# Queries and keys computed by features instead of by tokens, rotated by GpSimd and brought to the operands by DMA

## Chip, cores and metric
The kernel runs on one core of one Trainium2 chip. The metric is the device time of one execution in microseconds. The kernel before was timed in three runs; a fourth execution was recorded by the profiler.

## What is computed
Two sequences of 1024 tokens of width 512 (float32) pass six residual steps: an FFN with a LoRA term and a column norm, grouped attention with a rotary embedding (32 query heads, 8 key heads, 16 dimensions), the FFN again, a top-2 mixture of eight LoRA experts, a second attention (8 heads of 32 dimensions), and the experts again. Each step begins with a layer norm.

```
x = x + 0.5 * _L0_ffn_ref(_layernorm(x), ...)
x = x + _L0_attn_ref(_layernorm(x), ...)
x = x + 0.5 * _L0_ffn_ref(_layernorm(x), ...)
x = x + 0.5 * _L1_ffn_ref(_layernorm(x), ...)
x = x + _L1_attn_ref(_layernorm(x), ...)
x = x + 0.5 * _L1_ffn_ref(_layernorm(x), ...)
```

The rotation of the first attention takes the dimensions 2d and 2d + 1 of a head, xr and xi, to xr * cos - xi * sin and xr * sin + xi * cos.

## The kernel before
Each sequence passes eight stages (FFN_A, QKV0, WO0, FFN_B, MOE_A, QKV1, WO1, MOE_B) in three chains, with the rotated attention A0 after QKV0 and the standard attention A1 after QKV1. Every engine's program is written out by hand, in order, and engines meet by semaphores. Nothing is reordered later.

A chain handles eight tiles of 128 tokens per stage, in ticks. In tick i TensorE turns the normalised tile i to features by tokens (`turn_x`, L576), and multiplies tile i - 1 (`product`, `three_passes`, L596 to L598). Operands are split in a high and a low part of fp32r, so that a product has three passes; ScalarE copies the high part of the turned tile (L1080), the vector engine subtracts the low part (`turned_lo`, L844), takes statistics two tiles ahead (L825, L827), normalises the next tile (L837) and adds the product to x (`epilogue`, L872 to L879). GpSimd computes the inverse deviation (`rstd_of`, L1222, L1224), splits the weights of the next stage (`split_chunk`, L1215) and adds a bias (`bias_x`, L1235). In a tick of the experts the vector engine also routes (L887 to L891) and weighs (`weigh`, L898 to L910).

In QKV0 and QKV1 a product is 128 tokens by 768 features (two halves of 384 columns, L596 to L598). The vector engine adds the bias (L864) into one of three buffers. For A0 it multiplies by the cosine (L919), GpSimd by the sine in two strided instructions (L1254), and the vector engine adds (`rope_sum`, L932). ScalarE writes the high parts twice into a stack of 64 columns per head (`high_parts`, L1116, L1119), GpSimd subtracts the low parts beside them (`low_parts`, L1288, L1290) and copies the values (L1263). TensorE then turns the stacks, four blocks of 128 columns at a time (`turn_piece`, L654; five pieces per tile in A0, four in A1), four ticks behind the product, and ScalarE takes each piece to the operands (`evacuate`, L1137). An operand holds, per head, rows for high, low and again high (48 rows in A0, 96 in A1), and two more rows for the shift of the softmax.

Attention works in units of heads (8 units of 4 heads in A0, 4 of 2 in A1). For each unit a ring of three PSUM banks carries score maxima (TensorE L674, vector engine L976 and L980), the transposed shifts (L679, L989) and the normalisation of the result (L684, L996, L1001). The ring runs about one unit ahead of the scores (L759 in A1, L765 in A0), exponentials (ScalarE L1180), causal masks (GpSimd L1333) and value products (L781). 27 maximum banks of A0 and 21 of A1 stand ahead of the first score, twelve and six of them inside the chain's last ticks (`begun`). SP issues all DMAs in one queue: the shift rows go from `shiftT` to the operands (L495), weights from a copy in memory (`load_weights`).

## Time and profile before
| | |
|---|---|
| median of 3 runs | 1405.7 us (1405.19 to 1406.45) |
| profiled execution | 1411.57 us, span 1409.8 us |
| busy in the span | TensorE 1286.9 (91%), vector engine 943.4 (67%), ScalarE 639.8 (45%), GpSimd 483.3 (34%) |
| chain that ended last | TensorE 69%, vector engine 16%, GpSimd 5%, issue 4%, ScalarE 4%, DMA 2% |
| mean granted clock of TensorE | 0.929 |
| DMA queue of SP | 19312 packets, 38.23 MB, 8.0% of 16 engines |

The span runs from the first to the last instruction. Busy time is a sum of durations; matmuls are pipelined, so that a duration is longer than the distance from one matmul to the next. A share of the whole span is a mean of stages with different limits: what a stage is worth is read from windows of time. The granted clock is a share of TensorE's full speed, 0.5 being the lower of its two levels (1.2 of 2.4 GHz).

### The profile page before, as it was taken

Reading aid. Unit: us, or ns where it says so; the run is one execution under the profiler, and the core shown is the slowest. Engines: PE = TensorE matmul, PEld = TensorE weight load, DVE = VectorE, ACT = ScalarE, POOL = GpSimd, SP = SyncE. Lnnn points to the kernel's source line nnn. Section 1 sums busy time; section 2 is a strip of 40 time slices with the busy share of each in tenths; the row PEclk is TensorE's granted clock in tenths of the full one; section 3 lists DMA queues with packets and bytes.
Section 4 is the critical chain, followed back from the end, with each engine's and each line's share of the span. In section 5 each row is a group of like instructions: output and inputs, shape, how many; then the busy total and the mean of one; then the engine's idle time right before and its main releaser. Section 6 shows DMA issues by size and latency. Waiting matters only on the chain.

```text
span 1409.8 us, 21535 instructions
## 1 busy us (share of the span) xinstructions
PE 1286.9 (91%) x7392; PEld 824.5 (58%) x7392; DVE 943.4 (67%) x2782; ACT 639.8 (45%) x959; POOL 483.3 (34%) x733
## 2 busy tenths in 40 slices
PE   3988999999899998998979889999998999999988
PEld 1886543444268896444858854444432788954368
DVE  5664888999337944652857468889991587366356
ACT  1236266666632335444212544666665222544522
POOL 1574031221155542114626621321122554311162
PEclk9999588999999999899989976999999999989999
DMA  9200000001002001000140000000010100010001
GB/s 300 92 1 30 2 2 2 32 3 40 1 1 71 1 1 39 2 2 0 61 145 1 1 31 2 2 4 31 2 40 2 57 16 1 3 37 1 2 0 60
DMA packets 19420, 39.60 MB, mean 28 GB/s; under 512 B 4401, under 2 KB 5681, under 8 KB 19185
## 3 DMA queue, kind: packets, MB, share of 16 engines
q1 hardware_dynamic: 19312, 38.23, 8.0%
q8 instruction: 60, 0.98, 0.3%
q14 instruction: 48, 0.39, 0.1%
HBM read 32.33 MB, written 11.29 MB: 31 GB/s over the span
## 4 chain that ended last, share of the span: by engine, by line
PE 69%; DVE 16%; POOL 5%; issue 4%; ACT 4%; DMA 2%; SPq 0%; DVEq 0%; ACTq 0%; POOLq 0%
PE bank L781 16%; PE bank L674 12%; PE bank L596 8%; PE bank L598 7%; PE bank L597 7%; DVE maxes L980 5%; PE bank L765 4%; PE bank L654 4%; PE bank L759 3%; PE bank L576 3%; DVE unused L976 3%; PE bank L684 2%; POOL probs L1254 1%; DVE xT L844 1%; DVE gate L904 1%
## 5 line engine op out<-in xcount | busy, mean ns | idle before, releaser
L1180 ACT ACTIVATE probs<-bank 128x1024 f32<-128x1024 f32 (+3 forms) x416 | 367.9, 911 | 304.3 <-PE bank L765 195.6
L674 PE MATMUL bank<-ops 48*128 48x512 f32 (+3 forms) x960 | 321.0, 438 | 13.2 <-DVE maxes L980 3.8
L976 DVE CUSTOM_DVE_ANT_0 unused<-bank,causal 128x128 bf16<-128x128 f32 (+3 forms) x640 | 279.5, 486 | 73.9 <-PE bank L674 70.5
L1333 POOL TENSOR_SCALAR_AFFINE_SELECT probs<-probs 128x256 f32<-128x256 f32 (+1 forms) x256 | 118.8, 464 | 590.1 <-ACT probs L1180 589.9
L674 PEld LDWEIGHTS bank<-ops 48*128 48x128 f32 (+1 forms) x960 | 162.5, 207 | 198.2 <-DVE maxes L976 81.6
L781 PE MATMUL bank<-probs,v_mem 128*17 128x512 f32 (+6 forms) x1920 | 259.1, 531 | 6.1 <-ACT heads_raw L1169 5.6
L980 DVE TENSOR_REDUCE maxes<-bank 128x1 f32<-128x512 f32 x320 | 207.2, 684 | 38.0 <-PE bank L674 36.4
L1080 ACT CAST xT<-bank 128x512 fp32r<-128x512 f32 (+1 forms) x128 | 71.3, 560 | 280.5 <-PE bank L576 280.5
L844 DVE TENSOR_TENSOR xT<-bank,xT 128x512 fp32r<-128x512 f32 (+1 forms) x128 | 83.6, 656 | 148.4 <-ACT xT L1080 148.4
L765 PE MATMUL bank<-ops 50*128 50x512 f32 (+2 forms) x640 | 177.9, 454 | 4.1 <-ACT probs L1180 4.0
L596 PE MATMUL bank<-w_odd_hi,xT 128*128 128x384 f32 (+2 forms) x448 | 169.0, 377 | 2.1 <-DVE xT L844 1.9
L598 PE MATMUL bank<-w_odd_hi,xT 128*128 128x384 f32 (+2 forms) x448 | 152.8, 341 | 0.0
L597 PE MATMUL bank<-w_odd_lo,xT 128*128 128x384 f32 (+2 forms) x448 | 152.6, 341 | 0.0
L765 PEld LDWEIGHTS bank<-ops 50*128 50x128 f32 x640 | 87.3, 199 | 60.7 <-ACT probs L1180 30.8
L596 PE MATMUL bank<-ops,xT 128*128 128x512 f32 (+1 forms) x288 | 114.3, 397 | 5.3 <-DVE x L877 3.4
L1137 ACT CAST ops<-bank 128x512 fp32r<-128x512 f32 x144 | 81.7, 587 | 67.4 <-PE bank L654 67.0
L1222 POOL TENSOR_SCALAR var_eps<-mv 128x1 f32<-128x1 f32 x96 | 34.8, 363 | 202.3 <-DVE mv L827 202.3
L598 PE MATMUL bank<-ops,xT 128*128 128x512 f32 (+1 forms) x288 | 104.0, 361 | 0.0
L597 PE MATMUL bank<-ops,xT 128*128 128x512 f32 (+1 forms) x288 | 103.7, 360 | 0.0
L654 PE MATMUL bank<-identf,features 128*128 128x128 f32 x512 | 80.0, 293 | 22.1 <-POOL heads_raw L1290 16.1
L596 PEld LDWEIGHTS bank<-w_odd_hi,xT 128*128 128x128 f32 x448 | 85.8, 192 | 7.7 <-DVE xT L844 2.4
L597 PEld LDWEIGHTS bank<-w_odd_lo,xT 128*128 128x128 f32 x448 | 86.0, 192 | 3.5
(102 smaller groups left out, 1743.6 us busy)
## 6 DMA issues: line engine op xcount, KB each, us to landing
w_odd_lo<-staging_wqkv SPq DMA_DIRECT2D x4, 1536.0 KB, 6.7
x<-x_dram SPq DMA_DIRECT2D x16, 256.0 KB, 6.0
out_dram<-x SPq DMA_DIRECT2D x16, 256.0 KB, 2.0
staging_wqkv<-wqkv_dram SPq DMA_DIRECT2D x2, 1536.0 KB, 14.1
ops<-staging_dora SPq DMA_DIRECT2D x3, 1024.0 KB, 5.1
ops<-staging_base SPq DMA_DIRECT2D x2, 1296.0 KB, 6.4
w_odd_lo<-staging_base SPq DMA_DIRECT2D x2, 1296.0 KB, 5.8
ops<-shiftT SPq DMA_DIRECT2D x160, 4.0 KB
```

Of the source, the lines that this page charges most:

```text
L596: mm(dst, x_hi[:, k, :], hi[:, k, :], start=(k == 0), stop=False)
L597: mm(dst, x_hi[:, k, :], lo[:, k, :], start=False, stop=False)
L598: last = mm(dst, x_lo[:, k, :], hi[:, k, :], start=False, stop=(k == kc - 1 and not lora))
L654: last = nc.tensor.transpose(dst[:, k * P:(k + 1) * P], src, identf[:])
L674: last = mm(dst[:, h * w:(h + 1) * w], queries(a, u)[rows, t // 4, hi, t % 4 * P:(t % 4 + 1) * P], keys(a, u, hi)[rows, HALF * kp:HALF * k ...
L765: last = mm(dst, keys(a, u, 0)[rows, block], queries(a, u)[rows, c, heads_of[0]:heads_of[-1] + 1, columns], start=True, stop=True)
L781: last = mm(heads[a.head_rows * h:a.head_rows * h + a.dim + 1, q0 - HALF * c:HALF], v[:, j, a.kv_head(u, r, i), :], probs[:, e % 6, n, fir ...
L844: V.tensor_tensor(xT[:, n % 2, 1, 0:kc, :], turn[n % 2][:, 0:kc * P].rearrange("p (k c) -> p k c", k=kc), xT[:, n % 2, 0, 0:kc, :].bitcast ...
L976: V.tensor_tensor_reduce(unused[:, masked % 3, 0:w], part, causal[:, HALF - w:], 1.0, NEG, ALU.add, ALU.max, dst).then_inc(s["max_done"].s ...
L980: V.tensor_reduce(dst, part, AX.X, ALU.max).then_inc(s["max_done"].sem, 1)
L1180: A.activation(probs[:, e % 6, :, 0:cols], scores[:, 2 * (e % 2):2 * (e % 2) + 2, 0:cols], ACT.Exp, scale=a.scale).then_inc(s["exp"].sem, 1)
L1333: G.affine_select(out=p, in_=p, compare_op=ALU.is_ge, fill=0.0, base=0, pattern=pattern, channel_multiplier=-1).then_inc(s["masked"].sem, 1)
```

## The change
QKV0 and QKV1 no longer work by token tiles. `plan_chain` moves the turns of the attention stage into the preceding stage's last ticks (QKV0 begins four ticks before that stage's last product's tick, QKV1 three), and their high and low parts are kept for four tiles (`xT_group`), 512 tokens wide. A product (`heads_product`) is 128 features by 512 tokens with the weights as the stationary operand: (j, g) is feature block j of token half g, five blocks in A0 and four in A1. Values keep tokens as rows, one short product per tile; in A0 a pass over the high tokens takes both weight parts at once (256 columns). The features of A0 are sorted so that one block holds the real parts and the next the imaginary parts of 16 heads; block 0 holds both for the 8 key heads.

The vector engine reads each block of A0 out of PSUM four or two times (`heads_read`: bias and cosine, bias and sine), GpSimd makes both sums of the rotation (`rope_sums`, L520, L521), ScalarE the high part (`rope_high`), GpSimd the low part (`rope_low`, L1474). SP stores these rows to memory in six DMAs per rotation (`store_rope`) and loads the operands of keys and queries from there (`load_keys`, `load_queries`); three buffers hold the queries of units, the rest is loaded during attention. In A1 ScalarE and the vector engine write high and low parts of 32 lanes straight into the operands (`heads_high`, `heads_read`), and a DMA within SBUF copies the high part (`copy_high`). The stacks, their constants, the transposed pieces and their evacuation are gone; the rows of ones come by DMA.

In every chain the vector engine now takes the epilogue at the front of the tick. The experts' small transposes have a bank of their own, and WO1's weights are loaded after QKV1 and split during A1. Twelve ring items of either attention are now in the chain's ticks.

```diff
+    def plan_products(self):
+        first, second = [("v", t) for t in range(4)], [("v", t) for t in range(4, NT)]
+        if self.rope:
+            order = [(0, 0), (1, 0), (2, 0), first, (0, 1), (1, 1), (2, 1), (3, 0), (4, 0), (3, 1), (4, 1), second]
+            self.begun = {8: 3, 9: 6, 10: 9, 11: 12}
+        else:
+            order = [(0, 0), (1, 0), first, (3, 0), (0, 1), (1, 1), (3, 1), second, (2, 1), (2, 0)]
+            self.begun = {5: 2, 6: 4, 7: 6, 8: 9, 9: 12}
+        self.ticks = [item if isinstance(item, list) else [("qk", *item)] for item in order]
...
+def plan_chain(chain):
+    plain = [(st, t) for st in chain if st not in ATT for t in range(NT)]
+    ticks = [Tick([it], plain[n - 1] if n else None) for n, it in enumerate(plain)] + [Tick([], plain[-1])]
+    if chain[-1] in ATT:
+        st, a = chain[-1], ATT[chain[-1]]
+        early = len(plain) - (3 if chain[-2] in MOE_RANK else 4)
+        ticks += [Tick([], None, p) for p in a.ticks]
+        for t in range(NT):
+            ticks[early + t].turns.append((st, t))
+    elif chain[-1] in MOE_RANK:
+        ticks.append(Tick())
+    return ticks
...
+        def rope_sums(eng, ops_of, b, n):
+            s = qs[QKV0]
+            prods, _, _ = rope_set(n % 2)
+            m = rope_lanes[n]
+            eng.wait_ge(s["read"].sem, s["read"].at(b, A0.product_no("qk", *ropes[n]) + 1))
+            ops_of.tensor_tensor(prods[0:m, 0, :], prods[0:m, 0, :], prods[0:m, 3, :], ALU.subtract)
+            ops_of.tensor_tensor(prods[0:m, 1, :], prods[0:m, 1, :], prods[0:m, 2, :], ALU.add).then_inc(s["turned"].sem, 1)
...
+            def store_rope(b, n):
+                s, g, keys_only = qs[QKV0], 1 if n in (2, 3, 5) else 0, n in (0, 2)
...
+                lanes, rows = (64, k_rows) if keys_only else (P, q_rows[16 * (n // 4):16 * (n // 4) + 16])
...
+                sp.wait_ge(s["hi"].sem, s["hi"].at(b, n + 1))
+                for part in (0, 1 if keys_only else 2):
+                    for m in range(2):
+                        sp.dma_start(rows[part, m, :, :, HALF * g:HALF * (g + 1)], hi[0:lanes, m, :].bitcast(F32)
+                                     ).then_inc(rope_stored[n].sem, 16)
+                sp.wait_ge(s["lo"].sem, s["lo"].at(b, n + 1))
+                for m in range(2):
+                    sp.dma_start(rows[2 if keys_only else 1, m, :, :, HALF * g:HALF * (g + 1)], lo[0:lanes, m, :].bitcast(F32)
+                                 ).then_inc(rope_stored[n].sem, 16)
...
+            def load_queries(b, u, c):
+                n = 2 * c + 1 if u < 4 else 4 + c
+                sp.wait_ge(rope_stored[n].sem, rope_stored[n].at(b, 96))
+                into = queries_first if u == 0 and c == 0 else queries_in[u % 3]
+                for r in range(2):
+                    sp.dma_start(queries(A0, u)[64 * r:64 * r + A0.part_rows, c, :, :].bitcast(F32),
+                                 q_rows[4 * u:4 * u + 4].rearrange("(i r) p s -> r p i s", r=2)[r, :, :, HALF * c:HALF * (c + 1)]
+                                 ).then_inc(into.sem, 16)
+            def rotated_operands(b):
+                for g in range(2):
+                    store_rope(b, 2 * g)
+                    store_rope(b, 2 * g + 1)
+                    load_keys(b, g)
+                    load_queries(b, 0, g)
...
+            def rotated_attention(b):
...
+                load_shifts(b, QKV0, 0, 0)
+                load_shifts(b, QKV0, 0, 1)
+                store_rope(b, 4)
+                store_rope(b, 5)
                 for u in range(a.units):
+                    if u + 1 < a.units:
+                        load_shifts(b, QKV0, u + 1, 0)
+                        load_shifts(b, QKV0, u + 1, 1)
+                    if u + 3 < a.units:
+                        sp.wait_ge(s["scored"].sem, s["scored"].at(b, (u + 1) * a.unit_events))
+                        load_queries(b, u + 3, 0)
+                        load_queries(b, u + 3, 1)
+                    if u in (3, 4):
                         load_weights(b, FFN_B if u == 3 else MOE_A)
...
+            def heads_product(b, st, kind, j, g=0, between=None):
...
+                m = a.product_no(kind, j, g) if kind == "qk" else a.product_no(kind, j)
+                dst = qkv_banks[m % 3]
+                pe.wait_ge(xT_ready.sem, xT_ready.at(b, TURN_NO[st, 4 * g + 3 if kind == "qk" else j] + 1))
+                if m == 0:
+                    pe.wait_ge(w_ready.sem, w_ready.at(b, chunks_before(st + 1)))
+                elif m < 3:
+                    pe.wait_ge(x_new.sem, x_new.at(b, product_no(FFN_A if st == QKV0 else MOE_A, 7)))
+                else:
+                    pe.wait_ge(s["read"].sem, s["read"].at(b, m - 2))
...
+                if kind == "qk":
...
+                    for k in range(KC):
+                        mm(dst, hi[:, k, cols], x_hi[:, k, :], start=(k == 0), stop=False)
+                        mm(dst, lo[:, k, cols], x_hi[:, k, :], start=False, stop=False)
+                        last = mm(dst, hi[:, k, cols], x_lo[:, k, :], start=False, stop=(k == KC - 1))
+                else:
...
+                    if a.rope:
+                        both = w_odd.rearrange("p m (k n) -> p m k n", k=KC)[:, :, :, a.qk_feats:]
+                        wide = dst[:, 0:2 * n].rearrange("p (m n) -> p m n", m=2)
+                        for k in range(KC):
+                            if k < KC - 1:
+                                mm(wide, x_hi[:, k, :], both[:, :, k, :], start=(k == 0), stop=False)
+                            mm(dst[:, 0:n], x_lo[:, k, :], hi[:, k, a.qk_feats:], start=False, stop=False)
+                        last = mm(wide, x_hi[:, KC - 1, :], both[:, :, KC - 1, :], start=False, stop=True)
...
+                last.then_inc(s["product"].sem, 1)
...
-            def turn_piece(b, st, t, n):
...
-                dst = piece_bank(m, t)
-                for k in range(4):
...
-                    src = rows[:, a.row_tiles * h:a.row_tiles * (h + 1), :].rearrange("p h w -> p (h w)")
-                    last = nc.tensor.transpose(dst[:, k * P:(k + 1) * P], src, identf[:])
-                last.then_inc(s["piece"].sem, 1)
...
+            def heads_read(b, st, kind, j, g=0):
...
+                dve.wait_ge(s["product"].sem, s["product"].at(b, m + 1))
+                if kind == "v":
...
+                    into, bias = values(a)[:, j, :, 0:a.dim], bias_v[st][:, :]
+                    if a.rope:
+                        V.tensor_tensor(v_rest[:, j % 2, :], src[:, n:2 * n], bias, ALU.add).then_inc(s["rest"].sem, 1)
+                        dve.wait_ge(s["rest"].sem, s["rest"].at(b, j + 1))
+                        bias = v_rest[:, j % 2, :]
+                    V.tensor_tensor(into, src[:, 0:n].rearrange("p (h d) -> p h d", h=8),
+                                    bias.rearrange("p (h d) -> p h d", h=8), ALU.add).then_inc(s["read"].sem, 1)
+                elif a.rope:
...
+                    if n >= 2 and j in (0, 1, 3):
+                        dve.wait_ge(s["lo"].sem, s["lo"].at(b, n - 1))
+                    if j == 0:
+                        pieces = [(0, slice(0, 64)), (2, slice(64, P))]
+                    else:
+                        pieces = [(0 if j % 2 else 2, slice(0, P))]
+                    for first, lanes in pieces:
...
+                            last = V.scalar_tensor_tensor(prods[0:lanes.stop - lanes.start, first + i, :], src[lanes, :],
+                                                          bias_qk0[lanes, j:j + 1], table[lanes, :], ALU.add, ALU.mult)
+                    last.then_inc(s["read"].sem, 1)
+                else:
+                    dve.wait_ge(s["hi"].sem, s["hi"].at(b, sum(p[0] == "qk" for p in a.products[:m + 1])))
+                    for h in range(4):
+                        hi, lo = head_rows1(j, h, g)
+                        last = V.scalar_tensor_tensor(lo, src[32 * h:32 * (h + 1), :], bias_head1[:, 4 * j + h:4 * j + h + 1],
+                                                      hi.bitcast(F32), ALU.add, ALU.subtract)
...
+                    before = [ticks[i - n].product if 0 <= i - n < len(ticks) else None for n in (1, 2)]
+                    if before[1] is not None and before[1][0] in MOE_RANK:
+                        epilogue(b, *before[1])
+                    if before[0] is not None and before[0][0] not in MOE_RANK:
+                        epilogue(b, *before[0])
+                    for it in tick.turns:
+                        turned_lo(b, *it)
+                    for it in ticks[i + 2].turns if i + 2 < len(ticks) else ():
+                        statistics(b, *it)
+                    if experts:
+                        routing(b, *tick.product)
+                    for it in ticks[i + 1].turns if i + 1 < len(ticks) else ():
+                        normalise(b, *it)
+                    if experts:
+                        weigh(b, *tick.product)
+                    if tick.heads:
+                        for p in tick.heads:
+                            heads_read(b, att, *p)
+                        h = i - first_heads
+                        for n in range(ATT[att].begun.get(h - 1, 0), ATT[att].begun.get(h, 0)):
+                            ring_read(b, att, n)
...
+            def rope_high(b, n):
...
+                act.wait_ge(s["turned"].sem, s["turned"].at(b, n + 1))
+                if n >= 2:
+                    act.wait_ge(rope_stored[n - 2].sem, rope_stored[n - 2].at(b, 96))
...
+                A.copy(hi[0:m], prods[0:m, 0:2, :]).then_inc(s["hi"].sem, 1)
+            def heads_high(b, j, g):
...
+                act.wait_ge(s["product"].sem, s["product"].at(b, m + 1))
+                for h in range(4):
+                    hi, _ = head_rows1(j, h, g)
+                    last = A.activation(hi, qkv_banks[m % 3][32 * h:32 * (h + 1), :], ACT.Identity,
+                                        bias=bias_qk1[32 * h:32 * (h + 1), j:j + 1])
...
+            def rope_low(b, n):
...
+                pool.wait_ge(s["hi"].sem, s["hi"].at(b, n + 1))
...
+                G.tensor_tensor(lo[0:m], prods[0:m, 0:2, :], hi[0:m].bitcast(F32), ALU.subtract).then_inc(s["lo"].sem, 1)
...
+                    if st == QKV0 and g in (4, 6):
+                        rope_low(b, 4 + g // 6)
```

Where the instructions stand, at three places. First TensorE, in QKV0's fifth tick and later: L596 to L598 are the three passes of a product, L654 the transposes of a piece of the stacks. Before:

```order
L654 MATMUL bank<-identf,features 128x128 x4
L596 MATMUL bank<-w_odd_hi,xT 128x384
L597 MATMUL bank<-w_odd_lo,xT 128x384
L598 MATMUL bank<-w_odd_hi,xT 128x384
L654 MATMUL bank<-identf,features 128x128 x4
L596 MATMUL bank<-w_odd_hi,xT 128x384
L597 MATMUL bank<-w_odd_lo,xT 128x384
L598 MATMUL bank<-w_odd_hi,xT 128x384
```

Now, from the end of block (2, 0) into the first value tile (L793 to L795 are the passes of a block, L806 to L808 those of the values):

```order
L793 MATMUL bank<-ops,w_odd 128x512
L794 MATMUL bank<-ops,w_odd 128x512
L795 MATMUL bank<-ops,w_odd 128x512
L806 MATMUL bank<-w_odd,ops 128x256
L807 MATMUL bank<-w_odd,ops 128x128
L806 MATMUL bank<-w_odd,ops 128x256
L807 MATMUL bank<-w_odd,ops 128x128
L806 MATMUL bank<-w_odd,ops 128x256
L807 MATMUL bank<-w_odd,ops 128x128 x2
L808 MATMUL bank<-w_odd,ops 128x256
```

The transposes between the passes are gone, a pass is 512 wide, and the values are a run of short matmuls.

Second GpSimd, over the first three rotations of QKV0 (`features` holds the four products, `ops` the parts):

```order
L520 TENSOR_TENSOR features<-features 64x512
L521 TENSOR_TENSOR features<-features 64x512
L1474 TENSOR_TENSOR ops<-features,ops 64x1024
L520 TENSOR_TENSOR features<-features 128x512
L521 TENSOR_TENSOR features<-features 128x512
L1474 TENSOR_TENSOR ops<-features,ops 128x1024
L520 TENSOR_TENSOR features<-features 64x512
L521 TENSOR_TENSOR features<-features 64x512
L1474 TENSOR_TENSOR ops<-features,ops 64x1024
```

Where it had the sine's products, the low parts and the value copies of each tile, it has the sums and the low part of each rotation, one after the other.

Third the vector engine in a tick of MOE_A: `gate` and `route` are the gates, `top` the routing, `stats` and `mv` the statistics. Before:

```order
L844 TENSOR_TENSOR xT<-bank,xT 128x512
L825 BN_STATS stats<-x 128x6
L827 BN_AGGR mv<-stats 128x2
L887 MAX top<-bank 128x8
L889 MAX_INDEX top_at<-top,bank 128x8
L891 SCALAR_TENSOR_TENSOR x<-bank,x 128x188
L837 TENSOR_SCALAR probs<-x,mv,rstd 128x512
L872 SCALAR_TENSOR_TENSOR x<-bank,x 128x188
L874 SCALAR_TENSOR_TENSOR x<-bank,x 128x324
L898 TENSOR_SCALAR route<-route 128x1
L899 TENSOR_SCALAR gate<-expert_no,top_atf,route 128x8
```

Now, in a tick that also takes statistics for a tile of QKV1:

```order
L1062 SCALAR_TENSOR_TENSOR x<-bank,x 128x188
L1064 SCALAR_TENSOR_TENSOR x<-bank,x 128x324
L1051 TENSOR_TENSOR xT<-bank,xT 128x512
L1029 BN_STATS stats<-x 128x6
L1031 BN_AGGR mv<-stats 128x2
L1029 BN_STATS stats<-x 128x6
L1031 BN_AGGR mv<-stats 128x2
L1077 MAX top<-bank 128x8
L1079 MAX_INDEX top_at<-top,bank 128x8
L1081 SCALAR_TENSOR_TENSOR x<-bank,x 128x188
L1044 TENSOR_SCALAR probs<-x,mv,rstd 128x512
L1088 TENSOR_SCALAR route<-route 128x1
```

The epilogue (L872, L874; now L1062, L1064) moved from behind the normalisation to the front, and the turns of QKV1 bring a second set of statistics.

## Rows read from the trace of the kernel before

**Rows 1.** Busy time in windows: start:end, length, then PE, PEld, DVE, ACT, POOL, clock.
```profile
60.94:149.32 88.38, 76.67 (x433) 65.34 (x433) 51.38 (x115) 38.86 (x65) 46.27 (x60) 0.90 0.04 13
149.32:395.49 246.17, 233.95 (x1518) 98.25 (x1518) 196.31 (x669) 153.44 (x180) 53.71 (x102) 0.90 0.04 12
448.50:494.19 45.69, 43.52 (x276) 40.32 (x276) 41.33 (x121) 13.82 (x36) 26.22 (x37) 1.00 0.04 12
494.19:562.15 67.96, 62.93 (x382) 55.39 (x380) 31.64 (x81) 31.58 (x58) 21.79 (x37) 0.97 0.06 21
753.50:842.00 88.50, 76.83 (x434) 65.38 (x432) 50.71 (x114) 37.59 (x64) 46.25 (x61) 0.90 0.04 13
```

**Rows 2.** Waits from 61 to 129: who waited for whom, us, times, longest.
```profile
DVE probs L932 <- POOL heads_raw L1290: 13.6, 4, 3.9
```

**Rows 3.** Timeline of TensorE around QKV0: start, us, instruction, idle before it.
```profile
63.26 0.40 PE L597 MATMUL bank<-ops,xT 128*128 128x512 f32 x1
63.49 0.39 PE L598 MATMUL bank<-ops,xT 128*128 128x512 f32 x1
...
64.41 0.60 PE L576 MATMUL bank<-identf,probs 128*128 128x128 f32 x4
...
119.61 1.15 PE L654 MATMUL bank<-identf,features 128*128 128x128 f32 x8 [0.24 <-ACT ops L1137]
...
140.57 1.11 PE L674 MATMUL bank<-ops 48*128 48x512 f32 x2 [0.56 <-DVE maxes L976]
```

**Rows 4.** Groups of instructions by shape, vector engine: busy us, mean ns; idle before.
```profile
L844 DVE TENSOR_TENSOR xT<-bank,xT 128x512 fp32r<-128x512 f32 x112 | 77.1, 690 | 138.5 <-ACT xT L1080 138.5
L825 DVE BATCH_NORM_STATS2 stats<-x 128x6 f32<-128x512 f32 x96 | 65.6, 683 | 3.1 <-DMA x<-x_dram 3.1
L976 DVE CUSTOM_DVE_ANT_0 unused<-bank,causal 128x512 bf16<-128x512 f32 x160 | 103.4, 686 | 26.9 <-PE bank L674 26.9
L837 DVE TENSOR_SCALAR probs<-x,mv,rstd 128x512 f32<-128x512 f32 x96 | 53.1, 553 | 3.9 <-POOL rstd L1224 3.9
L976 DVE CUSTOM_DVE_ANT_0 unused<-bank,causal 128x128 bf16<-128x128 f32 x160 | 37.6, 288 | 19.8 <-PE bank L674 18.1
L879 DVE TENSOR_TENSOR x<-bank,x 128x512 f32<-128x512 f32 x32 | 21.9, 684 | 0.0
```

**Rows 5.** The same view, GpSimd.
```profile
L1215 POOL TENSOR_TENSOR w_odd_lo<-w_odd_lo,w_odd_hi 128x768 fp32r<-128x768 f32 x16 | 29.5, 1844 | 0.7 <-ACT w_odd_hi L1089 0.7
L1215 POOL TENSOR_TENSOR ops<-ops 128x512 fp32r<-128x512 f32 x16 | 20.6, 1286 | 19.6 <-ACT ops L1089 19.6
```

**Rows 6.** The same view, ScalarE.
```profile
L1137 ACT CAST ops<-bank 128x512 fp32r<-128x512 f32 x144 | 81.7, 587 | 67.4 <-PE bank L654 67.0
L1116 ACT CAST features<-probs 128x1024 fp32r<-128x1024 f32 x16 | 16.8, 1052 | 11.2 <-DVE probs L932 11.2
```

**Rows 7.** DMA issues: count, KB each, median us from issue to landing.
```profile
w_odd_lo<-staging_wqkv SPq DMA_DIRECT2D x4, 1536.0 KB, 6.7
out_dram<-x SPq DMA_DIRECT2D x16, 256.0 KB, 2.0
```

**Rows 8.** Timeline in MOE_A, and L837's shortest, median and longest in ns.
```profile
467.74 1.29 POOL L1235 TENSOR_TENSOR x<-x,bbase 128x512 f32<-128x512 f32 x1
467.84 1.21 DVE L904 SCALAR_TENSOR_TENSOR gate<-expert_no,top_atf,gate 128x8 f32<-128x8 f32 x1
...
489.54 0.23 DVE L904 SCALAR_TENSOR_TENSOR gate<-expert_no,top_atf,gate 128x8 f32<-128x8 f32 x1
...
L837 DVE TENSOR_SCALAR probs<-x,mv,rstd x96: 515/532/1476, 21.0 to 1391.9; 128x512 f32<-128x512 f32 x96
```

**Rows 9.** Busy time in windows, columns as in rows 1 (clock third from last).
```profile
61.00:69.00 8.00, 7.97 (x45) 7.15 (x45) 5.46 (x11) 1.17 (x2) 3.85 (x11) 1.00 0.00 0
142.00:149.00 7.00, 6.50 (x16) 3.77 (x16) 6.85 (x26) 0.00 (x0) 0.00 (x0) 0.50 0.01 2
149.30:187.00 37.70, 36.78 (x158) 18.14 (x158) 31.81 (x105) 16.60 (x19) 3.73 (x9) 0.60 0.01 2
```

809 lines of the change are left out of this document (414 added, 395 removed).

## Prediction

> **What bounds the kernel now.** I read the busy time stage by stage first. The kernel alternates between token-tiled chains and two attentions. The reader should see in [rows 1] that TensorE is busy nearly everywhere, and that two stretches per sequence are spent on making queries and keys: from the first turn of QKV0 to the first score, 60.94 to 149.32 (88.4 us), and from the turn of QKV1's second tile to the first score, 494.19 to 562.15 (68.0 us). The second sequence repeats the first of them at 88.5 us, and I take it to repeat the second as well: 313 us of 1410 together. The rotated attention itself, 246 us per sequence, is left as it is.
>
> The waits of the rotated stretch come next. The vector engine's sum L932 waits for GpSimd's low parts [rows 2], and ScalarE waits for the transposed pieces [rows 6]: each tile goes round a loop of all engines, and TensorE's transposes of the stacks (L654) are both work and the end of that loop. In the timeline of TensorE [rows 3] a 512-column matmul follows the last after 0.23 us; eight 128-column transposes take 1.15 us (0.12 to 0.14 us each); the tick of the first QKV0 product opens at 64.41; and the first maximum bank after the twelfth is read at 140.57, so that the rest of the ring's lead takes 8.75 us up to the score at 149.32. The vector engine sets that last part: sixteen instructions of 0.29 to 0.69 us per twelve banks [rows 4].
>
> **Removed.** The piece transposes: 8 x 20 in QKV0 and 8 x 16 in QKV1, at 0.12 us 19 and 15 us of TensorE per sequence, with ScalarE's evacuations behind them, GpSimd's strided products and value copies, and the vector engine's L864, L919 and L932. The round trip per tile goes as well.
>
> **Rotated heads, now.** Four of QKV0's turns move into ticks of FFN_A. A tick there takes 3.35 us by TensorE. The vector engine has 2.6 us in it by the rows' durations (0.69 turned + 0.68 statistics + 0.55 normalise + 0.68 sum), some 0.2 for the short instruction between statistics and normalisation, and another turn adds up to 2.1 [rows 4]. Neighbouring instructions overlap by about 0.1, so a double tick is near 4.5 us: +1.1 for four ticks. I take +4, and the first product starts at 64.4 + 4 = 68.4.
> - TensorE: ten products of 12 x 0.23 = 27.6 us; the values of eight tiles, 64 short matmuls at 0.12 to 0.14 (as the transposes), 8; three turns 1.4; sixteen matmuls of twelve maximum banks 2.7. Sum 39.7.
> - Vector engine: 24 reads of 512 columns of PSUM at 0.69 (as L879) = 16.6; 16 short ones near 0.3 = 5; three turns 6; sixteen maxima, mean of both ends 0.49, 7.8. Sum 35, below TensorE.
> - GpSimd: twelve sums of 512 at 1.29 = 15.5, six low parts of 1024. From 512 (1.29) to 768 (1.84) is 2.1 ns per element [rows 5], so 1024 takes 2.4. Two low parts lie in attention: 25 us here. One rotation's path is 2.6 (sums) + 1.05 (ScalarE, 1024) [rows 6] + 2.4 = 6.0 us, and even six in full would be 36, just under 39.7.
> - DMA: the fourth rotation starts near +25 and ends near +31. Then come a store (2.0 us for 256 KB), 0.8 MB of keys and 0.4 MB of queries, between 2.0 and 6.7 us [rows 7], so the second half's operands land at +37 to +41; the thirteenth bank wants them at +39.7. The first score also needs its shift rows, now queued behind 1.6 MB of queries and 1 MB of weights: at 1.5 MB in 6.7 us they land near +51 against +48.4. For both I take 3.5, between 0 and 8.
>
> First score at 68.4 + 39.7 + 8.75 + 3.5 = 120.4 instead of 149.3: 29 us per sequence, 58 in all. Bounds: 34 (DMA hidden) and 19 (see the first rival).
>
> Here the choice of GpSimd is to be weighed. The row shows 1.29 us for a two-input instruction of 512, against 0.69 on the vector engine. The Trainium skill ("GPSIMD Engine Reference", Engine selection) gives the same factor of about two and advises the vector engine for such work. By that rule the twelve sums would be 8.3 us there, and the vector engine at 43 us would pass TensorE's 39.7; by the rows GpSimd's 25 us stay beneath it, so I price the sums at nothing as long as the 6.0 us path keeps up.
>
> **A lock between the two.** In [rows 8] L904, eight elements, takes 1.21 us and ends with GpSimd's L1235; without GpSimd at work it takes 0.23. That instruction reads two SBUF tensors. The new reads take PSUM, a pointer and one table, like L879, whose mean stays 0.68: price 0. The Trainium skill ("Advanced Engine Details and Errata", Mode Summary) also has two-port instructions blocked by GpSimd. By that the three normalisations beside rotations would each wait up to 1.3 us, 4 us per sequence; their row's mean, 0.55, hardly shows it.
>
> The same lock prices something else. The expert epilogue (L872 and L874, together 512 columns of PSUM, near 0.68 us by L879 [rows 4]; I take 0.66) moves from between statistics and gates, where GpSimd's lock covered it, to the front of the tick. Where GpSimd also splits weights, the tick grows by 0.66. Four such ticks of MOE_A make 2.6 us per sequence, counted with QKV1 below; four of MOE_B in the first sequence 2.6 and about 1 in the second, together the 3.6 of the sum.
>
> **Standard heads, now.** The four double or early turns of QKV1 fall into MOE_A ticks that the vector engine already fills (41.3 of 45.7 us busy, [rows 1]): the turns need 4 x (0.69 + 0.68 + 0.55) = 7.7 us there and a gap of 4.4 takes part of it, but some of them wait out GpSimd's lock; I take +5, and with the 2.6 above +7.6, so the heads start at 494.2 + 7.6 = 501.8. TensorE: 96 x 0.23 = 22.1, values 96 x 0.13 = 12.5, turns 1.9, ring 3: 39.5. Vector engine: 32 reads of 32 x 512 at 0.69 = 22.1 (32 lanes priced as 128), values 3.4, turns 7.5, ring 8: 41. ScalarE 32 x 0.6 = 19, but ahead of the vector engine's reads, so about 5 us of filling. First score at 501.8 + 46 + 8 = 555.8 against 562.15: 6.4 us per sequence, 12.8 in all; between 16 gained (no filling, ring hidden for half) and 6 lost (ScalarE and vector engine one after the other for half of the blocks) per sequence.
>
> Priced at nothing: the queries of later units, loaded one unit (246 / 8 = 31 us) ahead against landings of up to 6.7; the stores of the last two rotations, which stand on SP's queue before the shift rows of the second unit, since they wait only for the first unit's seventh step of twelve; their two high and two low parts in that unit, where TensorE is the bound; the copies of high parts between partitions, two products ahead of their first reader; and WO1's load and split, which move behind QKV1 and into attention, where GpSimd is idle for most of the time. Without their cover each would cost its own landing, 2 to 7 us per sequence.
>
> **Sum.** -58 - 12.8 + 3.6 = -67.2 us. The profiled execution took 1411.6 us, so 1344.4 by it; the three runs' median lies 5.9 below it, so I forecast 1339.
>
> **Rivals.**
> - The GpSimd path is the bound. The two sums, ScalarE's copy and the low part are serial, every rotation's buffers wait for the low part two earlier, and a margin of 4 us over six rotations is thin; memory trips may take the longer row. Then the operands are some 10 us late per sequence: gain 2 x 19 + 12.8 - 3.6 = 47, 1359. For it: a normalisation took 1.48 us at worst beside GpSimd [rows 8], so the engines do collide; against: fifteen us lie between the fourth rotation's product and the bank that wants it. Chance 0.18.
> - The clock. From 142 us the granted clock is 0.50, and 0.60 over 149.3 to 187 [rows 9], right after TensorE had waited on the ring. If TensorE comes to attention busy and the clock holds, 37.7 us shrink to 37.7 x 0.6 = 22.6, 15 us per sequence: 1309. Against: the vector-bound tail of 8.75 us before the scores is still there. Chance 0.12.
> - Slower: the clock falls inside the new heads stages. TensorE's waits for ScalarE, GpSimd or DMA there could put dense products at half clock, each costing 0.46 instead of 0.23. The four stages hold 158 us of TensorE work, and what runs at half clock takes twice as long; once 43% of it does, the 67 us are gone, and at 60% the time is 1339 + 95 = 1434. For it: the granted clock of 61 to 149 is already 0.90 with such waits [rows 1]; against: the end of FFN_A and the first products of QKV0, just as dense, keep 1.00 [rows 9]. Chance 0.05, with 0.01 for landing on no change.
>
> **The numbers.** My forecast has 0.64. The range takes in both first rivals with a few us of error in TensorE's sums: 1306 to 1374. About 0.2% (3 us) is what a measurement of this kernel can tell from no change. Faster 0.94, same 0.01, slower 0.05.
>
> **What would show it.** Right: the first score near 120 and 555 us, L807-like short matmuls 0.12 to 0.14 apart, GpSimd's sums 1.3 us, MOE_A ticks with splits near 6.6 us instead of 5.9, no wait over 4 us for key or query rows, attention of 246 us. Wrong: TensorE waiting for DMA of query rows, granted clock under 0.9 in the heads stages, or attention shorter than 235 us by its clock.

## Result, and the profile after

The changed kernel takes **1394.8 us** (median of 4 runs, 1391.8 to 1396.0), against 1406.1 for the kernel before beside it: a ratio of 0.990 (95% interval 0.986 to 0.994). Forecast were 1339 and a range of 1306 to 1374. It is faster, as forecast, but by 11 us, under 1%, instead of 67. A ratio is worked out from the executions in the faster of two states that a kernel shows, while a median and a range take in all, so that a ratio is not quite the quotient of two medians (0.992 here). The profiled execution has a span of 1392.6 us against 1409.8. The stages, from the starts of turns and scores in the two timelines, first and second sequence (the last MOE_B runs to the end of the span):

| us | before | changed | forecast of the difference | measured |
|---|---|---|---|---|
| first turn of FFN_A to first rotated score | 126.1, 117.6 | 103.5, 96.4 | -29, -29 | -22.6, -21.2 |
| rotated attention | 246.2, 246.4 | 248.2, 248.5 | 0 | +2.0, +2.1 |
| WO0 and FFN_B | 53.0, 51.4 | 50.8, 52.4 | 0 | -2.2, +1.0 |
| first turn of MOE_A to first standard score | 113.7, 113.8 | 121.2, 120.8 | -6.4, -6.4 | +7.6, +7.0 |
| standard attention | 91.6, 89.1 | 89.1, 88.8 | 0 | -2.5, -0.3 |
| MOE_B | 52.8, 49.1 | 61.6, 53.0 | +2.6, +1.0 | +8.8, +3.9 |

So the gain in QKV0 is there, 44 us of the 58 forecast. 27 us of it are given back in MOE_A with QKV1 and in MOE_B, where 9 were expected to be gained. (The differences, with the 0.7 us by which the first turn comes earlier, add up to the 17 us between the two spans; WO1 takes the same in both and is left out.) The windows of the changed kernel that answer to [rows 1] (QKV0, rotated attention, MOE_A, QKV1, MOE_B; columns as there):

```profile
69.67:126.08 56.41, 47.99 (x231) 36.52 (x229) 42.14 (x111) 7.14 (x8) 26.06 (x19) 0.91 0.68 173
126.08:374.23 248.15, 233.65 (x1517) 98.85 (x1517) 197.07 (x666) 155.38 (x182) 58.60 (x104) 0.90 0.16 40
425.10:482.44 57.34, 48.62 (x292) 45.05 (x292) 51.92 (x136) 14.26 (x39) 28.59 (x38) 0.94 0.00 1
482.44:546.28 63.84, 49.44 (x240) 40.52 (x238) 44.95 (x95) 24.41 (x37) 2.02 (x4) 0.84 0.23 63
653.30:714.90 61.60, 46.47 (x271) 42.47 (x271) 43.29 (x122) 11.59 (x36) 23.33 (x31) 0.91 0.21 72
```

The fourth row is the odd one: no engine is full. TensorE has 49 of 64 us, the vector engine 45, ScalarE 24. Something makes them take turns. MOE_B shows the same, 46 and 43 of 62.

The durations that the prediction used hold within 0.1 us. The groups by shape (sums of both sequences), GpSimd's sums and low parts, the reads of QKV0 and QKV1, ScalarE's high parts:

```profile
L520 POOL TENSOR_TENSOR features<-features 128x512 f32<-128x512 f32 x8 | 10.3, 1284 | 10.1 <-DVE features L1138 10.1
L1474 POOL TENSOR_TENSOR ops<-features,ops 128x1024 fp32r<-128x1024 f32 x8 | 19.0, 2370 | 12.0 <-ACT ops L1344 12.0
L1138 DVE SCALAR_TENSOR_TENSOR features<-bank,bias_qk,probs 128x512 f32<-128x512 f32 x16 | 12.0, 749 | 13.6 <-PE bank L795 8.9 <-POOL ops L1474 4.5
L1145 DVE SCALAR_TENSOR_TENSOR ops<-bank,bias_head,ops 32x512 fp32r<-32x512 f32 x64 | 47.8, 747 | 24.2 <-ACT ops L1354 23.2
L1354 ACT ACTIVATE ops<-bank,bias_qk 32x512 fp32r<-32x512 f32 x64 | 43.6, 681 | 34.9 <-PE bank L795 34.2
```

The sums take 1.28 us (priced 1.29), a low part 2.37 (2.4), a read 0.75 (0.69), a high part 0.68 (0.6). What the prediction counted at 5 us per sequence stands behind the bar of L1145: 23.2 us over both in which the vector engine waits for ScalarE.

Two waits on transfers are left in QKV0. The timeline of TensorE, first maximum bank and first score:

```profile
100.02 0.72 PE L860 MATMUL bank<-ops 48*128 48x128 f32 x6 [1.95 <-DMA ops<-query_rows_dram]
126.08 0.80 PE L970 MATMUL bank<-ops 50*128 50x512 f32 x2 [2.42 <-DMA ops<-shiftT]
```

And this is a tick of MOE_A, vector engine first, then TensorE's next product and GpSimd's split:

```profile
436.54 0.15 DVE L1088 TENSOR_SCALAR route<-route 128x1 f32<-128x1 f32 x1
436.60 1.76 DVE L1089 TENSOR_SCALAR gate<-expert_no,top_atf,route 128x8 f32<-128x8 f32 x1
438.28 0.15 DVE L1092 RECIPROCAL route<-route 128x1 f32<-128x1 f32 x1
438.40 1.19 DVE L1094 SCALAR_TENSOR_TENSOR gate<-expert_no,top_atf,gate 128x8 f32<-128x8 f32 x1
439.70 0.35 DVE L1100 SCALAR_TENSOR_TENSOR hw_mem<-bank,route,gate 128x128 f32<-128x128 f32 x1
439.96 0.34 DVE L1062 SCALAR_TENSOR_TENSOR x<-bank,x 128x188 f32<-128x188 f32 x1
440.23 0.48 DVE L1064 SCALAR_TENSOR_TENSOR x<-bank,x 128x324 f32<-128x324 f32 x1
```
```profile
440.86 0.61 PE L768 MATMUL bank<-ops,xT 128*128 128x324 f32 x1 [2.80 <-DVE x L1064]
```
```profile
436.51 1.83 POOL L1440 TENSOR_TENSOR w_odd<-w_odd 128x768 fp32r<-128x768 f32 x1
438.30 1.27 POOL L1461 TENSOR_TENSOR x<-x,bbase 128x512 f32<-128x512 f32 x1
```

TensorE has turned its tile at 437.46 and waits 2.80 us for the epilogue (L1064), which stands behind the gates. The gates are long because GpSimd works beside them: L1089 and L1094, eight elements each, end with L1440 and L1461; the shortest of the 32 executions of L1089 took 0.27 us, half of them 1.18 and more. In the kernel before the epilogue stood ahead of the gates.

### The profile page after: what moved, and what is told of

Its sections match the earlier page's. It is cut to its first block, busy times and chain, and to the rows that moved or that the text cites. A ratio compares the mean times of both kernels' runs of the same rounds, so it can differ in the third digit from the quotient of the medians.

```text
span 1392.6 us, 21472 instructions
## 1 busy us (share of the span) xinstructions
PE 1222.2 (88%) x6800; PEld 754.3 (54%) x6800; DVE 1008.2 (72%) x2878; ACT 573.1 (41%) x827; POOL 433.1 (31%) x617
## 4 chain that ended last, share of the span: by engine, by line
PE 61%; DVE 24%; issue 5%; ACT 4%; DMA 3%; POOL 1%; SPq 1%; DVEq 0%; ACTq 0%; POOLq 0%
PE bank L986 16%; PE bank L860 12%; PE bank L768 5%; PE bank L970 4%; PE bank L770 4%; PE bank L769 4%; DVE maxes L1206 4%; PE bank L964 3%; PE bank L754 3%; DVE probs L1044 3%; DVE unused L1202 2%; DVE ops L1145 2%; PE bank L870 2%; DVE stats L1029 2%; DVE gate L1089 2%
## 5 line engine op out<-in xcount | busy, mean ns | idle before, releaser
L1202 DVE CUSTOM_DVE_ANT_0 unused<-bank,causal 128x128 bf16<-128x128 f32 (+3 forms) x640 | 279.7, 486 | 44.9 <-PE bank L860 41.2
L1313 ACT CAST xT<-bank 128x512 fp32r<-128x512 f32 (+1 forms) x96 | 52.5, 551 | 231.5 <-PE bank L754 231.5
L768 PE MATMUL bank<-ops,xT 128*128 128x512 f32 (+1 forms) x288 | 116.3, 404 | 23.7 <-DVE x L1064 18.1
L970 PEld LDWEIGHTS bank<-ops 50*128 50x128 f32 x640 | 88.1, 200 | 64.1 <-issue 31.4
L769 PE MATMUL bank<-ops,xT 128*128 128x512 f32 (+1 forms) x288 | 105.6, 367 | 0.0
L770 PE MATMUL bank<-ops,xT 128*128 128x512 f32 (+1 forms) x288 | 105.6, 367 | 0.0
L754 PE MATMUL bank<-identf,probs 128*128 128x128 f32 x384 | 61.0, 288 | 49.3 <-DVE probs L1044 49.0
L768 PE MATMUL bank<-w_odd,xT 128*128 128x324 f32 (+1 forms) x192 | 74.4, 387 | 13.5 <-DVE x L1064 11.5
L1051 DVE TENSOR_TENSOR xT<-bank,xT 128x512 fp32r<-128x512 f32 (+1 forms) x96 | 61.4, 643 | 33.6 <-ACT xT L1313 33.6
L986 PEld LDWEIGHTS bank<-probs,v_mem 128*17 128x17 f32 (+1 forms) x1920 | 40.9, 99 | 78.6 <-issue 53.6
L754 PEld LDWEIGHTS bank<-identf,probs 128*128 128x128 f32 x384 | 44.6, 144 | 69.4 <-DVE probs L1044 67.7
L1225 DVE RECIPROCAL inv_sum<-bank 128x16 f32<-128x16 f32 (+1 forms) x48 | 11.3, 235 | 95.1 <-PE bank L870 95.0
L768 PEld LDWEIGHTS bank<-ops,xT 128*128 128x128 f32 x288 | 56.7, 197 | 34.4 <-issue 20.6
L1029 DVE BATCH_NORM_STATS2 stats<-x 128x6 f32<-128x512 f32 x96 | 65.2, 679 | 3.3 <-DMA x<-x_dram 3.3
```

What stands on the lines that cost most here:

```text
L754: last = nc.tensor.transpose(turn[n % 2][:, k * P:(k + 1) * P], src[:, k * P:(k + 1) * P], identf[:])
L768: mm(dst, x_hi[:, k, :], hi[:, k, :], start=(k == 0), stop=False)
L769: mm(dst, x_hi[:, k, :], lo[:, k, :], start=False, stop=False)
L770: last = mm(dst, x_lo[:, k, :], hi[:, k, :], start=False, stop=(k == kc - 1 and not lora))
L970: last = mm(dst, keys(a, u, 0)[rows, block], queries(a, u)[rows, c, heads_of[0]:heads_of[-1] + 1, columns], start=True, stop=True)
L986: last = mm(heads[a.head_rows * h:a.head_rows * h + a.dim + 1, q0 - HALF * c:HALF], v[:, j, a.kv_head(u, r, i), :], probs[:, e % 6, n, fir ...
```

## Experiments

Three kernels were built one on another (e1 the epilogue, e7 the shift rows, e8 the hand-over); the others are side steps. Each ratio is against the kernel before, run beside it. Stages are read from one profiled execution each. The kernels that don't touch QKV0 (the changed one twice, e1, e3, e4, e5) spread by themselves in the stretch from FFN_A's first turn to the first rotated score: 102.4 to 106.9 us in the first sequence, 95.0 to 99.5 in the second.

**The epilogue's place.** e1 puts only the experts' epilogue back:

```diff
-                    if before[1] is not None and before[1][0] in MOE_RANK:
-                        epilogue(b, *before[1])
...
                         normalise(b, *it)
+                    if before[0] is not None and before[0][0] in MOE_RANK:
+                        epilogue(b, *before[0])
                     if experts:
                         weigh(b, *tick.product)
```

> The changed kernel (profiled span 1392.6 us) with the experts' epilogue moved back behind the normalisation and ahead of the weights of the gates, in the tick after its product; nothing else. Theory 1, loop: TensorE may not begin the product of tile t + 1 before the epilogue of tile t - 1 has freed its banks; at the front of the next tick the epilogue stands behind the gates (L1089, L1094), so product, routing, gates and epilogue follow one another in a ring. Then the ticks of MOE_B that take 8.6 to 9.4 us fall to 5 to 6.5, MOE_B's 61.6 us of the first sequence to about 53 and the 53.0 of the second to about 49, MOE_A gives 3 to 5 per sequence: 20 to 24 us in all, near 1371. Theory 2, lock alone, as in the prediction: only the 0.66 us that stood under GpSimd's lock comes back in each tick with a split, 8.8 us in all, near 1386.

Measured: 1369.0 us (1367.9 to 1375.9), ratio 0.972 (0.967 to 0.977). MOE_B takes 52.6 and 48.4 us, MOE_A up to QKV1 51.8 and 52.2 instead of 57.0 and 57.0. (QKV1 is taken here and below to begin with the turn of a tile that TensorE makes 0.35 us ahead of the first block.) TensorE's instructions and their order are the same in both. The windows of e1's MOE_A and its two MOE_B:

```profile
426.40:478.10 51.70, 47.59 (x288) 42.95 (x288) 48.24 (x131) 15.59 (x39) 27.99 (x38) 0.97 0.01 1
649.70:702.30 52.60, 43.17 (x270) 39.30 (x270) 39.43 (x122) 12.32 (x36) 23.20 (x31) 0.95 0.25 86
1319.40:1367.80 48.40, 42.50 (x270) 39.41 (x270) 33.92 (x117) 10.11 (x32) 16.86 (x23) 0.98 0.12 44
```

GpSimd's work is the same as in the changed kernel (23.2 us in MOE_B), yet the stage is 9 us shorter. 25 us came back (24 of them in these four stages), the ring's figure and not the 8.8 of the lock alone. The gates are shorter too, since the epilogue now stands between them and the normalisation: half of L1089's executions take 0.48 us or less.

**GpSimd's part in it.** e4 leaves out GpSimd's split of the weights of QKV1 and of the second FFN_A instead, all but one column:

```diff
-                A.copy(weights(st, 0)[:, k, :], weights(st, 1)[:, k, :].bitcast(F32)).then_inc(w_hi_ready.sem, 1)
+                if st in (QKV1, FFN_A):
+                    A.activation(weights(st, 0)[:, k, :], weights(st, 1)[:, k, :].bitcast(F32), ACT.Copy, scale=0.0
+                                 ).then_inc(w_hi_ready.sem, 1)
+                else:
+                    A.copy(weights(st, 0)[:, k, :], weights(st, 1)[:, k, :].bitcast(F32)).then_inc(w_hi_ready.sem, 1)
...
+                c = slice(0, 1) if st in (QKV1, FFN_A) else slice(None)
-                G.tensor_tensor(lo, lo.bitcast(F32), hi.bitcast(F32), ALU.subtract).then_inc(w_ready.sem, 1)
+                G.tensor_tensor(lo[:, c], lo[:, c].bitcast(F32), hi[:, c].bitcast(F32), ALU.subtract).then_inc(w_ready.sem, 1)
```

> The changed kernel, leaving out GpSimd's subtraction of the low parts of the weights of QKV1 and of the second sequence's FFN_A (one column of each chunk is still made; the high part is written as zero, so that the products stay finite). It prices GpSimd's lock in the ticks of the experts. Loop theory: the gates still stand ahead of the epilogue, so the ticks fall by the 1.8 us of the split at most and stay above 6 us (MOE_B of the second sequence, which has no split, has 5.0 to 6.6). Lock theory: without the split the ticks are at 5.0 to 5.3 us as before. Total between 10 and 16 us faster than the changed kernel by the first, over 20 by the second.

Measured: one run, 1375.9 us. The ticks of MOE_B's last products in the first sequence start at 661.2, 667.8, 673.5, 679.4 and 686.2, 5.7 to 6.8 us apart, above the 5.3 of the kernel before, so the ring stays without the split. The total gained 19 us where 10 to 16 were expected; but only 16.8 of it lie in the stages that the edit touches (5.9 us in each MOE_A, 4.9 in the first MOE_B, none in the second), QKV1 gave back 1.7, and most of the rest of the gain is the rotated attention, which the edit doesn't touch (245.2 and 245.1 us instead of 248.2 and 248.5). Twelve ticks hold a split, eight of 1.83 and four of 1.28 us, 20 us in all; so most of it was on the path. Taking away either cause gives back 17 to 24 us in these stages, and the two are not added: GpSimd's lock is dear because it lies in the ring. GpSimd still adds its bias beside the gates in e4 (half of L1089's executions take 1.19 us or more), and no run takes all of its work away, so what the ring alone would cost isn't shown.

**Who makes the sums.** e2 gives them to the vector engine:

```diff
                             heads_read(b, att, *p)
+                            if att == QKV0 and p[1:] in ropes:
+                                rope_sums(dve, V, b, ropes.index(p[1:]))
...
-                    if att == QKV0:
-                        for p in tick.heads:
-                            if p[1:] in ropes:
-                                rope_sums(pool, G, b, ropes.index(p[1:]))
```

> The changed kernel with the twelve sums of the rotation made by the vector engine right behind its reads of the block, instead of by GpSimd. If the path sums, copy, low part, store, load is what delays the thirteenth maximum bank (TensorE waits 1.95 us for query rows there), the rotation's path falls from 6.0 to about 4.8 us, the wait goes and up to 2 us per sequence are gained. If the vector engine's time counts (it takes 12 x 0.69 = 8.3 us more per sequence, and sets the ring's tail), the first score comes up to 8 us later per sequence. As only four of the six rotations end before the tail and two sums of the last stand beside the ring, I expect the first score within 3 us of 126.1, and the total from 3 us faster to 8 slower. GpSimd as the bound of the rotation (the first rival of the prediction) would show as over 8 us gained.

Measured: 1398.3 us (1390.8 to 1400.3), ratio 0.991 (0.988 to 0.995). The stretch to the first rotated score takes 106.6 and 98.0 us, 3.1 and 1.7 more than in the changed kernel, which is within the spread given above. So it isn't shown that either engine is the better place; but the first rival has fallen: over 8 us should have come back, and the quicker path gained nothing. By the Trainium skill ("GPSIMD Engine Reference", Engine selection) the vector engine should have them; per instruction the trace agrees (0.68 to 0.85 us in e2 against 1.28), but the time of the kernel doesn't show it.

**Values first, and values between.** e3 moves the first four value tiles ahead of the first block of QKV1:

```diff
-            order = [(0, 0), (1, 0), first, (3, 0), (0, 1), (1, 1), (3, 1), second, (2, 1), (2, 0)]
+            order = [first, (0, 0), (1, 0), (3, 0), (0, 1), (1, 1), (3, 1), second, (2, 1), (2, 0)]
```

> The changed kernel with the values of the first four tiles as the first item of QKV1, ahead of the blocks (0, 0) and (1, 0), instead of behind them. In the changed kernel TensorE waits 4.70 us at 494.31 for a normalisation (L1044) that stands on the vector engine behind the four reads of block (0, 0), which in their turn wait for ScalarE's four high parts. With the value products there, whose reads are short, the normalisations of the last tiles don't stand behind a block's reads. Theory: this wait goes, 3 to 5 us gained per sequence, 6 to 10 in all. Rival: the vector engine has 41 us of work in this stretch anyway and the wait returns later, at the first maxima (3.4 us at 518.5, 3.3 at 536.2): under 2 us in all.

Measured: 1392.9 us (1390.6 to 1402.6), ratio 0.989 (0.986 to 0.992). MOE_A to first score stays at 121.2 and 120.1: the theory's 6 to 10 us did not come, and the rival holds. The wait for a normalisation is still there, 3.85 us at 498.68. e5 spreads the values, and the maximum banks with them, on top of e1:

```diff
-            order = [(0, 0), (1, 0), first, (3, 0), (0, 1), (1, 1), (3, 1), second, (2, 1), (2, 0)]
+            order = [(0, 0), first[:2], (1, 0), first[2:], (3, 0), (0, 1), second[:2], (1, 1), second[2:], (3, 1), (2, 1), (2, 0)]
-            self.begun = {5: 2, 6: 4, 7: 6, 8: 9, 9: 12}
+            self.begun = {5: 2, 6: 3, 7: 4, 8: 6, 9: 7, 10: 9, 11: 12}
```

> On top of the kernel with the experts' epilogue moved back (1369.0 us): in QKV1 the eight value products stand in pairs between the blocks, (0,0) v0 v1 (1,0) v2 v3 (3,0) (0,1) v4 v5 (1,1) v6 v7 (3,1) (2,1) (2,0), and the twelve maximum banks are spread to fit. In that kernel the stretch from QKV1's first block to the first score takes 64.2 us although TensorE is busy for 50.4, the vector engine for 45.9 and ScalarE for 24.4: none is full. Theory: the order clumps the vector engine's work (four value tiles with short reads in a row, then blocks with four reads of 0.75 us each, behind ScalarE's four copies of 0.69); spread evenly, 4 to 9 us are gained per sequence, 8 to 18 in all, and TensorE's wait of 4.7 us for a normalisation goes. Rival: the wait for the block's reads is the same wherever the values stand (moving them to the front gained 1 us in all), and the total stays within 3 us of 1369.

Measured: 1386.4 us (1384.4 to 1388.9), ratio 0.980 (0.974 to 0.987), against 0.972 for e1. My theory was wrong in its sign: QKV1 takes 69.6 and 69.5 us up to the first score instead of 64.1 and 62.9. TensorE's waits in it, from e5's timeline, say why:

```profile
507.62 0.47 PE L793 MATMUL bank<-ops,w_odd 128*128 128x512 f32 x1 [2.78 <-DVE ops L1145]
518.27 0.36 PE L811 MATMUL bank<-w_odd,ops 128*128 128x256 f32 x1 [1.43 <-DVE ops L1145]
521.33 0.47 PE L793 MATMUL bank<-ops,w_odd 128*128 128x512 f32 x1 [1.21 <-DVE ops L1145]
```

A block that stands alone shows its whole hand-over: ScalarE's four copies and then the vector engine's four reads, one after the other. In the changed kernel two lines show one of them, ScalarE's copies and the reads behind them:

```profile
529.47 2.77 ACT L1354 ACTIVATE ops<-bank,bias_qk 32x512 fp32r<-32x512 f32 x4 [11.71 <-PE bank L795]
```
```profile
532.34 3.03 DVE L1145 SCALAR_TENSOR_TENSOR ops<-bank,bias_head,ops 32x512 fp32r<-32x512 f32 x4 [4.03 <-ACT ops L1354]
```

Over both sequences the vector engine waits for these copies 23.2 us in six waits in the changed kernel and 41.1 us in ten in e5.

**The hand-over itself.** e8 signals every high part, on top of e7 (below); the changed counts of the signal are left out here:

```diff
-                    dve.wait_ge(s["hi"].sem, s["hi"].at(b, sum(p[0] == "qk" for p in a.products[:m + 1])))
                     for h in range(4):
+                        dve.wait_ge(s["hi"].sem, s["hi"].at(b, 4 * blocks_before + h + 1))
...
-                    last = A.activation(hi, qkv_banks[m % 3][32 * h:32 * (h + 1), :], ACT.Identity,
-                                        bias=bias_qk1[32 * h:32 * (h + 1), j:j + 1])
-                last.then_inc(s["hi"].sem, 1)
+                    A.activation(hi, qkv_banks[m % 3][32 * h:32 * (h + 1), :], ACT.Identity,
+                                 bias=bias_qk1[32 * h:32 * (h + 1), j:j + 1]).then_inc(s["hi"].sem, 1)
```

> On top of the kernel with the epilogue moved back and the shift rows sent early (1363.6 us): in QKV1 ScalarE signals each of a block's four high parts, and the vector engine takes each low part as soon as its own high part is there, instead of waiting for all four (2.8 us). Theory: the 64.2 us from QKV1's first block to the first score hold several hand-overs (first block, block (3,0) after the values, block (3,1) after the second values) where the vector engine stands still while ScalarE makes four copies of 0.69; each becomes 2.1 us shorter, 4 to 8 us gained per sequence, 8 to 16 in all, and the wait of 4.7 us for a normalisation shrinks by about 2. Rival: the vector engine's 45 us are what counts and the hand-overs only move: under 3 us in all.

Measured: 1359.0 us (1346.1 to 1366.6, 6 runs), ratio 0.959 (0.955 to 0.962). From first block to first score 57.1 and 58.1 us instead of 64.2 and 62.9: 7.1 and 4.8, within the theory's 4 to 8. The vector engine's waits for the copies fall to 8.4 us in four waits over both sequences. In its timeline the reads of the first block (L1147 there) begin 1.6 us after ScalarE's first copy instead of 2.9:

```profile
481.95 2.80 ACT L1356 ACTIVATE ops<-bank,bias_qk 32x512 fp32r<-32x512 f32 x4 [1.19 <-PE bank L796]
```
```profile
483.55 3.02 DVE L1147 SCALAR_TENSOR_TENSOR ops<-bank,bias_head,ops 32x512 fp32r<-32x512 f32 x4
```

e10 is e8 with e5's order of values:

> On top of the kernel with the hand-over head by head (1359.0 us; 57.1 and 58.1 us from QKV1's first block to the first score): the value products in pairs between the blocks again. With the whole-block hand-over this order made the stretch 5.4 and 6.8 us longer (69.6 against 64.2 and 62.8). Theory: a block that stands alone between values shows its whole hand-over (product, ScalarE's copies, the vector engine's reads one after another), and this order has more such blocks; with the short hand-over the loss shrinks by 2.1 us per exposed block, to 0 to 4 us per sequence. Rival: the order costs by something else, the banks or the later ring, and the loss stays at 5 to 7 us per sequence.

Measured: 57.2 and 58.2 us, the same as e8; the loss of 5 to 7 us is gone entirely. So the order cost through the hand-over, as the theory had it (its estimate was 0 to 4 us left). The total is 1353.7 us (1348.4 to 1365.5), ratio 0.964 (0.959 to 0.970), not distinct from e8.

**The shift rows.** e7, on top of e1:

```diff
                 load_shifts(b, QKV0, 0, 1)
+                load_queries(b, 2, 0)
+                load_queries(b, 2, 1)
+                load_weights(b, WO0)
...
-                for u in (1, 2):
-                    load_queries(b, u, 0)
-                    load_queries(b, u, 1)
-                load_weights(b, WO0)
+                load_queries(b, 1, 0)
+                load_queries(b, 1, 1)
                 rotated_attention(b)
```

> On top of the kernel with the epilogue moved back (1369.0 us): on SP's queue the queries of the third unit and WO0's weights are issued behind the shift rows of the first unit instead of ahead of them. In the changed kernel SP is busy issuing ten query loads from 107.4 to 116.3, the shift rows go out at 117.3 and TensorE waits 2.42 us for them at 126.1 (1.34 in the second sequence). Theory: the rows land behind 1.6 MB of queries and 1 MB of weights; issued ahead of half of it they land in time, and 1.3 to 2.4 us are gained per sequence, 3 to 5 in all. Rival: the low clock follows the wait wherever it is and the attention takes the gain back, or the third unit's queries come late: within 1 us.

Measured: 1363.6 us (1358.9 to 1375.3), ratio 0.966 (0.958 to 0.974), 5.5 less than e1, though the two intervals overlap. The stretch to the first rotated score takes 100.8 and 92.6 us, 2.9 and 3.9 less than in e1, without a wait at its end; e8 and e10, which keep the edit, have 101.1 and 100.1, 92.2 and 92.7, all below the spread given above. In the profiled execution the first sequence's rotated attention then takes 253.5 instead of 247.5, the second's 245.1 instead of 248.1. A unit between the first and the last takes 28.3 us at a granted clock of 1.00 and 30.6 at 0.89, and which units are slow differs from kernel to kernel, so that two or three us of one execution's attention are not told apart. The SP queue shows what stood ahead: ten issues of queries ahead of the rows, in the changed kernel:

```profile
107.36 8.90 SPq L630 DMA_DIRECT2D ops<-query_rows_dram  x10
116.30 0.43 SPq L579 DMA_DIRECT2D w_odd<-staging_wo  x1
117.32 3.20 SPq L597 DMA_DIRECT2D ops<-shiftT  x4
```

In e7 six such issues stand there, and the rows go out at the same time, 117.30. So the wait was not for the place in the queue: with the third unit's queries and WO0's weights out of the way, the rows had landed by 123.07, the first score there, and before only at 126.08.

**The ring later.** e9, on top of e7, has `self.begun = {9: 4, 10: 8, 11: 12}` in QKV0.

> On top of the kernel with the epilogue moved back and the shift rows sent early (1363.6 us): the first maximum banks of QKV0 stand one tick later, behind the block (4, 0) instead of (3, 0), four, four and four instead of three each. TensorE waits 1.95 us there for the queries of the first unit (store, load from memory). Theory: the wait is hidden by the next block and 1 to 2 us are gained per sequence. Rival: the vector engine's tail sets the first score, and the maxima start later on it: 0 to 3 us lost per sequence.

Measured: 1388.2 us, four runs widely spread (1370.7 to 1397.1), ratio 0.984 (0.980 to 0.988); the profiled execution's span is 1369.0 against 1363.6. In it the first score comes 6.9 and 5.0 us later, more than even the rival's 0 to 3. The wait for the query rows is gone, but TensorE now waits for the vector engine's maxima (L1203 there) 4.9 and 4.6 us in three waits each, where e7 had none and one of 0.7. So the wait on query rows cost less than a later start of the maxima.

**The clock.** e6, on top of e1, adds two products behind each of the tail's ring items:

```diff
-                ring_items(len(a.ring_first) - count["ring"])
+                for _ in range(len(a.ring_first) - count["ring"]):
+                    ring_items(1)
+                    if st == QKV0:
+                        for _ in range(2):
+                            mm(bank[:, 0, :], xT[:, 1, 0, 0, :], xT[:, 1, 0, :, :], start=True, stop=True)
```

> On top of the kernel with the epilogue moved back (1369.0 us): behind each maximum bank of the tail before the rotated scores (16 ring items per sequence) TensorE also makes two 512-column products into a bank that nothing reads, 0.23 us each at full clock, so that it doesn't wait for the vector engine there. It tests the prediction's second rival: if the clock falls because TensorE waits in the tail, it now stays near 1.00 and the first unit of the attention, 44 to 45 us at 0.61, comes down towards 30: 10 to 15 us gained per sequence, 20 to 30 in all. If the clock falls for all that (as a busy engine's clock also does at times in the attention: 0.89 over 855 to 916), the tail's items take 3 x 0.45 us instead of the vector engine's 0.69 and the kernel is 5 to 20 us slower in all.

Measured: 1400.7 us (1387.1 to 1411.4), ratio 0.984 (0.975 to 0.993) against e1's 0.972. The stretch to the first rotated score takes 117.9 and 112.8 us instead of 103.7 and 96.5, the first unit still 42.6 and 43.0 (44.9 and 44.9 in e1). Windows ahead of the score, of the changed kernel and of e6, and e6 from there on:

```profile
110.00:126.00 16.00, 10.94 (x38) 6.40 (x37) 13.98 (x47) 0.00 (x0) 1.29 (x2) 0.70 0.86 193
110.00:126.00 16.00, 15.21 (x45) 7.95 (x44) 9.28 (x33) 0.00 (x0) 1.27 (x2) 0.69 0.81 191
126.00:171.00 45.00, 43.18 (x138) 20.91 (x137) 31.32 (x99) 13.58 (x15) 7.60 (x8) 0.50 0.22 69
```

TensorE is busy for 15.2 of 16 us instead of 10.9, and the granted clock falls as in the changed kernel (0.69 against 0.70 over the same window) and stays at its lower level longer, to 170.8 us, though TensorE is busy for 43.2 of the last 45. The second rival has fallen, and with it its reason for this stretch: with nearly all of the tail's waits for the vector engine filled the clock was no higher. Waits before the tail are left in e6, so the run doesn't say that waits have no part. The Trainium skill ("TensorE: Matmul & The Clock Gate", What's actually happening) has the lower level as the state of an engine without activity, which work releases; by that these products should have held or released the clock, and the run doesn't agree. What lowers it here wasn't found.

**The changed kernel once more:**

> The changed kernel once more, nothing edited, beside the others on the same chip, since the kernel before has read between 1405 and 1413 us from call to call. Both theories expect the ratio found first, 0.990, within its interval (0.986 to 0.994).

Measured: 1398.1 us (nine runs), ratio 0.992 (0.990 to 0.995), inside the first interval.

## Why the prediction was wrong

By the profiled executions the forecast missed by 50 us. Of these 17 lie in the ticks of the experts (8 in MOE_A, 9 in MOE_B), 19 in the heads of QKV1, and 14 in QKV0 with the ticks of FFN_A ahead of it.

- **The lock moves with the epilogue: +0.66 per tick.** This step failed. It asked what the moved instructions cost on the vector engine and not who waits for them. TensorE's product of tile t + 1 needs the banks that the epilogue of tile t - 1 frees. At the front of the tick that epilogue stands behind the gates, and product, routing, gates and epilogue became one ring: from turn to turn up to 9.5 us, not 6.6. Price: 12.7 us in MOE_B against the 3.6 forecast, and in MOE_A 57.4 us to the first block, twice, where 53.3 was forecast; e1 took back 25 in all, and its 52.1 and 52.6 us to the first block leave 6.4 and 6.9 for the turns, which the prediction had priced at 5.
- **Heads from 501.8 to 555.8, 46 + 8 us.** This step failed too, by the filling. The vector engine's own work was nearly right (41, measured 45); the filling of 5 us was counted once, but each block behind values, and the first, pays ScalarE's 2.8 us before the vector engine starts: 11.6 us of waits in the first sequence. The stretch took 63.8 and 63.4 us instead of 54. e8 took 7.1 and 4.8 of that back; the rest I can't assign by a run. The clock has a part in it, the third rival's: it was 0.84 in the first sequence's stretch, and it fell at 491.9, 519.2 and 536.2, each time beside a wait of TensorE of 3.3 to 4.7 us. TensorE was busy for 15.7 us at the lower level, where value products of 256 columns follow each other after 0.21 us and not 0.12, so by these two about 7 us of its work are the clock's, an estimate; how much of that lay on the path isn't shown. Four tiles of values took 7.4 us so, 0.15 per product and not 0.13.
- **QKV0: 29 us per sequence.** Right in mechanism, forecast too large: 22.6 and 21.2 measured. TensorE's products ended 42.3 us after the first (69.67 to 112.0), waits of 1.33 and 1.95 included, so 39.0 of work against 39.7. The start was 1.3 late. The tail was mis-sized: 14.1 us from there to the score, where 8.75 and a share of the 3.5 for transfers were given. 2.4 of it is the wait for the shift rows, a cost that the prediction named and e7 took away; TensorE also waits 1.3 and 0.9 us for the vector engine's maxima, which I take for a backlog that the engine brought into the tail; no run tests that.
- **GpSimd: price nothing, while the 6.0 us path keeps up.** Nothing in e2 speaks against it: taking the sums off GpSimd gained nothing.
- **The lock on normalisations.** By the Trainium skill ("Advanced Engine Details and Errata", Mode Summary) they would wait for GpSimd, and the prediction held their row against it. In the rotated stages the prediction was nearly right: one normalisation per sequence is long there, 0.98 us beside L520. In the ticks of the experts the trace sides with the rule: thirteen more take 1.0 to 2.06 us, all beside an instruction of GpSimd, and L1044's mean rose from 553 to 682 ns. That adds 0.129 x 96 = 12 us of vector engine time over both sequences, of which I can't say how much lay on the path.
- **Rivals.** GpSimd's path (0.18) and the clock held high (0.12) were both wrong, and the third (0.05) came in part, without making the kernel slower. What mattered most had no case of its own: an order on the vector engine that makes TensorE wait.

## What to carry to other kernels

When an instruction moves on its engine, list the engines that wait for its signal, not only what it costs there; a buffer that is freed behind a slow step joins that step to the next product. Count a filling once for every place where the pipeline drains, and signal in the smallest piece that the next engine can use. Both are what these runs showed for this kernel. A version with the epilogue ahead of the gates, the shift rows early and the hand-over head by head takes 1359.0 us, ratio 0.959, 3% under the changed kernel.

## What I had not expected of the hardware

How completely a small instruction waits out GpSimd: L1089, eight elements, took 1.76 us beside the split that had begun 0.09 us before it, where the prediction had read 1.21. Blocks of 32 lanes cost the vector engine as much each as blocks of 128 (0.75 us both), as the prediction had assumed, and ScalarE 0.68 us against 0.59 for its copy of 128 lanes. And TensorE's clock fell over the same stretch with the engine busy for 15.2 of 16 us as with it busy for 10.9 (0.69 and 0.70).
